# Cross attentions: ScalarE instead of VectorE copies the turned weighted sums, the outputs and, in the first one, the shift rows out of PSUM

## The reference

```python
def cross_of_layer_0(x, y):                  # heads of 32, softmax over 1500 context rows
    xn = ln(x) * lnx_g + lnx_b
    yn = ln(y) * lny_g + lny_b               # y is ctx_512
    q = einsum('bsc,hcd->bhsd', xn, wq)
    k = einsum('btc,hcd->bhtd', yn, wk)
    v = einsum('btc,hcd->bhtd', yn, wv)
    a = softmax(einsum('bhsd,bhtd->bhst', q, k) * 32 ** -0.5)
    o = einsum('bhst,bhtd->bhsd', a, v)
    ...                                      # output matrix, then an MLP

def cross_of_layer_1(q, k, v):               # heads of 8, k = v = ctx_512, with biases
    qh, kh, vh = (q @ Wq + bq), (k @ Wk + bk), (v @ Wv + bv)
    attn = softmax(einsum('bhqd,bhkd->bhqk', qh, kh) * 8 ** -0.5)
    return einsum('bhqk,bhkd->bhqd', attn, vh) @ Wo + bo
```

## Time and profile before

| | |
|---|---|
| median of 3 runs | 655.38 us (655.01 to 655.65) |
| the profiled execution | 658.64 us |
| its span | 656.8 us |
| `cross1`, first to last exponential | 120.1 to 317.2 us |
| `cross2`, first to last exponential | 424.6 to 619.7 us |
| PE busy | 612.1 us, 93% |
| DVE busy | 496.9 us, 76% |
| POOL busy | 380.3 us, 58% |
| ACT busy | 349.6 us, 53% |

### The profile page before, as it was taken

How to read it: one execution, slowest core, us unless ns; L and a number is a source line. 1 busy time by engine, 2 the same in 40 slices (tenths; PEclk the granted TensorE clock), 3 DMA queues, 4 the chain that set the end, 5 groups by cost and what they waited for, 6 DMA issues and landing times.

```text
span 656.8 us, 19531 instructions
## 1 busy us (share of the span) xinstructions
PE 612.1 (93%) x8614; PEld 458.6 (70%) x8614; DVE 496.9 (76%) x795; ACT 349.6 (53%) x540; POOL 380.3 (58%) x272
## 2 busy tenths in 40 slices
PE   9688898899999999999899889899999999999997
PEld 4466775677777777777776556677777777777864
DVE  3776738799989989896657764877988988988543
ACT  2245663655646646647263326276576586664442
POOL 1542453388888888574220325078988988955400
PEclk9879999999999999999899999999999999999998
DMA  4820003000000002000024000001101100000000
GB/s 162 232 122 2 4 1 136 1 2 2 2 2 2 2 3 96 3 2 2 1 84 170 1 0 1 1 2 49 49 2 50 49 2 2 2 2 2 2 1 15
DMA packets 4656, 20.85 MB, mean 32 GB/s; under 512 B 500, under 2 KB 756, under 8 KB 4572
## 3 DMA queue, kind: packets, MB, share of 16 engines
q1 hardware_dynamic: 4572, 19.60, 8.9%
HBM read 19.37 MB, written 0.23 MB: 30 GB/s over the span
## 4 chain that ended last, share of the span: by engine, by line
PE 71%; DVE 13%; ACT 8%; issue 5%; POOL 2%; DMA 1%; POOLq 0%; DVEq 0%; ACTq 0%
PE psum L1155 18%; PE psum L1053 10%; PE psum L1096 5%; PE psum L1103 5%; PE psum L1098 5%; PE psum L213 3%; DVE scratch L1277 3%; PE psum L1032 3%; PE psum L244 1%; PE psum L1072 1%; ACT scratch L1195 1%; POOL scratch L648 1%; PE psum L1059 1%; PE psum L1066 1%; ACT scratch L1193 1%
## 5 line engine op out<-in xcount | busy, mean ns | idle before, releaser
L1262 POOL TENSOR_TENSOR scratch<-scratch 125x896 bf16<-125x896 f32 x136 | 239.4, 1770 | 114.5 <-ACT scratch L1242 114.5
L1242 ACT ACTIVATE scratch<-psum 125x896 f32<-125x896 f32 x192 | 173.2, 915 | 146.4 <-PE psum L1155 145.2
L1277 DVE TENSOR_REDUCE scratch<-psum 128x1 f32<-128x500 f32 x336 | 209.9, 671 | 13.9 <-PE psum L1053 6.4
L1155 PE MATMUL psum<-scratch 128*125 128x448 bf16 (+2 forms) x624 | 143.7, 355 | 0.7 <-ACT scratch L1242 0.2
L1096 PE MATMUL psum<-tok,scratch 125*128 125x65 bf16 x1344 | 108.7, 195 | 2.3 <-DVE kT L1322 1.8
L1098 PE MATMUL psum<-tok,scratch 125*128 125x64 bf16 x1344 | 108.2, 192 | 0.0
L1096 PEld LDWEIGHTS psum<-tok,scratch 125*128 125x128 bf16 x1344 | 95.7, 97 | 15.5 <-issue 2.6
L1053 PE MATMUL psum<-scratch 128*128 128x500 bf16 x273 | 102.2, 375 | 3.1 <-DVE scratch L1277 2.0
L1098 PEld LDWEIGHTS psum<-tok,scratch 125*128 125x128 bf16 x1344 | 90.1, 98 | 16.1
L1155 PEld LDWEIGHTS psum<-scratch 128*125 128x125 bf16 (+2 forms) x624 | 79.6, 136 | 26.8 <-DVE scratch L1289 1.3
L1262 DVE TENSOR_TENSOR scratch<-scratch 125x896 bf16<-125x896 f32 x56 | 70.6, 1268 | 15.1 <-ACT scratch L1242 14.7
(11 more groups left out here) (340 smaller groups left out, 906.5 us busy)
## 6 DMA issues: line engine op xcount, KB each, us to landing
nrm<-turned_dram SPq DMA_DIRECT2D x8, 750.0 KB, 4.4
raw<-ctx_dram SPq DMA_DIRECT2D x4, 672.0 KB
w_third<-fifth_dram SPq DMA_DIRECT2D x3, 636.0 KB, 5.4
w_third<-third_dram SPq DMA_DIRECT2D x2, 844.0 KB, 8.4
w_third<-third_dram SPq DMA_DIRECT2D x2, 843.5 KB, 6.8
w_fourth<-fourth_dram SPq DMA_DIRECT2D x3, 542.5 KB, 5.9
w_first<-first_dram SPq DMA_DIRECT2D x1, 996.0 KB, 4.9
w_second<-second_dram SPq DMA_DIRECT2D x1, 834.5 KB, 6.9
```

What stands on the lines that cost most here:

```text
L1155: mm = nc.tensor.matmul(bank(S + f, HALF, CP), lhs[0:rows, CP * c:CP * c + CP], rhs[0:rows, HALF * f:HALF * f + HALF], start=(rows == 128) ...
L1242: nc.scalar.activation(CR["p"][0:CP, n % RING, :].rearrange("p (f n) -> p f n", f=2), psum[0:CP, S:S + 2, 0:HALF], ACT.Exp).then_inc(self. ...
L1262: ops.tensor_tensor(CR["pl"][0:CP, n % RING, :], CR["p"][0:CP, n % RING, :], p_high(n % RING), ALU.subtract).then_inc(done, 1)
L1277: nc.vector.tensor_reduce(mxp[:, r, t:t + 1], bank(B, TB), X_AXIS, ALU.max).then_inc(self.aux_freed, 1)
```

## The change

The readers of some units change engine, and with them the semaphore that frees the unit.

- N and O are read by ACT in both attentions (`on_act`, `copy_act`). The scale and bias of `cross1` go into the same ACT instruction.
- A is read by ACT in `cross1`; in `cross2` it stays with DVE.
- ACT does a unit where it does its units of that chunk: N and N behind the exponential of c = 3, O behind that of c = 5 (and behind the exponential alone, since `context_act` stands at c = 4 and 6), A and A behind that of c = 11. At the end of each attention it does the last N, N and O.
- A new semaphore `act_freed` counts what ACT has freed of these, and the waits of PE and POOL on such a unit count on it.
- The matmuls are the same ones in the same order.

```diff
+            def on_act(self, u):
+
+                return u[0] in ("NO" if self.biased else "NOA")
...
+                elif self.on_act(u):
+                    eng.wait_ge(self.act_freed, self.freed_by_act(idx))
...
+            def copy_act(self, act, u, idx, b):
+
+                kind, k = u
+                B, i = self.home(idx), b % 2
+                lo, hi = (0, 512) if k == 0 else (512, 896)
+                act.wait_ge(self.aux_ready, idx + 1)
+                if kind == "A":
+                    nc.scalar.activation(CR["qb", i][64:65, lo:hi], psum[64:65, B, 0:hi - lo], ACT.Copy
+                                         ).then_inc(self.act_freed, 1)
+                elif kind == "N":
+                    if k == 0 and b:
+                        act.wait_ge(self.aux_ready, self.index("O", 0, b - 1) + 1)
+                    if self is cross1:
+                        ins = nc.scalar.activation(usb[0:64, lo:hi], bank(B, hi - lo, 64), ACT.Identity,
+                                                   bias=col("lnyb", 0, 64), scale=col("lnyg", 0, 64))
+                    else:
+                        ins = nc.scalar.activation(usb[0:64, lo:hi], bank(B, hi - lo, 64), ACT.Copy)
+                    ins.then_inc(self.mean_turned, 1)
+                else:
+                    nc.scalar.activation(oT[:, :, 56 * b:56 * b + 56],
+                                         psum[:, B, 0:224].rearrange("p (j t) -> p j t", t=56), ACT.Copy
+                                         ).then_inc(self.act_freed, 1)
...
                     for unit in units:
                         self.act_unit(act, *unit)
+                for unit in self.last:
+                    self.act_unit(act, *unit)
...
-                elif kind == "N":
-                    dve.wait_ge(self.aux_ready, idx + 1)
...
-                        ins = nc.vector.tensor_copy(usb[0:64, lo:hi], bank(B, hi - lo, 64))
-                    ins.then_inc(self.mean_turned, 1)
-                elif kind == "O":
-                    dve.wait_ge(self.aux_ready, idx + 1)
-                    nc.vector.tensor_copy(oT[:, :, 56 * b:56 * b + 56],
-                                          psum[:, B, 0:224].rearrange("p (j t) -> p j t", t=56)
-                                          ).then_inc(self.aux_freed, 1)
...
-                for unit in self.last:
-                    self.dve_unit(dve, *unit)
...
+            for u in FRONT[-2:]:
+                cross1.copy_act(act, u, cross1.index(*u, 0), 0)
             cross1.run_act(act)
```

More of the change, by code:

```diff
@@ L952, in __init__ @@
                 self.tag, self.src, self.wk, self.wv, self.biased = tag, src, wk, wv, biased
[L953 removed]
+                (self.aux_ready, self.aux_freed, self.act_freed, self.scores, self.probs, self.pv_done, self.mean_turned, self.tok_high,
                  self.tok_set, self.ya_set, self.yb_set, self.q_high, self.max_set, self.rec_set, self.mean_set, self.low_dve,
@@ L956, in __init__ @@
                     sem(f"{tag}_{n}") for n in (
-                        "aux_ready", "aux_freed", "scores", "probs", "pv", "mean_turned", "tok_high", "tok_set",
+                        "aux_ready", "aux_freed", "act_freed", "scores", "probs", "pv", "mean_turned", "tok_high", "tok_set",
                         "ya_set", "yb_set", "q_high", "max_set", "rec_set", "mean_set", "low_dve", "low_pool",
@@ L977, in __init__, with freed_by_act @@
                 self.order += [(u, b) for u, _, b in self.last]
+            def on_act(self, u):
+                return u[0] in ("NO" if self.biased else "NOA")
             def freed(self, idx):
-                return sum(u[0] not in "TN" and (u[0], b) != ("Q", 0) for u, b in self.order[:idx + 1])
+                return sum(u[0] not in "TN" and not self.on_act(u) and (u[0], b) != ("Q", 0) for u, b in self.order[:idx + 1])
+            def freed_by_act(self, idx):
+                return sum(u[0] != "N" and self.on_act(u) for u, b in self.order[:idx + 1])
             def home(self, idx):
@@ L1168, in run_pe @@
                     pe.wait_ge(self.probs, CHUNKS * BATCH)
-                    projection(0, [HALVES[0]], self.aux_freed, self.freed(done))
-                    projection(1, [slice(N // 2, N - SEQ)], self.aux_freed, self.freed(done))
+                    projection(0, [HALVES[0]], self.act_freed, self.freed_by_act(done))
+                    projection(1, [slice(N // 2, N - SEQ)], self.act_freed, self.freed_by_act(done))
                 if projection is None:
@@ L1189, in act_unit @@
                     if k == 0 and b >= 2:
-                        act.wait_ge(self.aux_freed, self.freed(self.index("A", 1, b - 2)))
+                        self.wait_freed(act, self.index("A", 1, b - 2))
                     cols = slice(HALF * k, HALF * k + HALF)
@@ L1285, in dve_unit @@
                     shift, below = CR["qb", i][64:65, lo:hi], psum[64:65, B, 0:hi - lo]
-                    if self.biased:
-                        if b < 2:
-                            dve.wait_ge(y_ones, 7)
-                        nc.vector.tensor_tensor(shift, below, CR["qb", i][96:97, lo:hi], ALU.subtract
-                                                ).then_inc(self.aux_freed, 1)
-                    else:
-                        nc.vector.tensor_copy(shift, below).then_inc(self.aux_freed, 1)
+                    if b < 2:
+                        dve.wait_ge(y_ones, 7)
+                    nc.vector.tensor_tensor(shift, below, CR["qb", i][96:97, lo:hi], ALU.subtract
+                                            ).then_inc(self.aux_freed, 1)
                 elif kind == "T":
@@ L1351, in front_dve_run @@
                         self.front_low_dve(dve, 1)
-                    self.dve_unit(dve, u, k + self.turns + 2, 0)
+                    if not self.on_act(u):
+                        self.dve_unit(dve, u, k + self.turns + 2, 0)
             def run_dve(self, dve, projected=None):
@@ L1356, in run_dve @@
                     b, c = n // CHUNKS, n % CHUNKS
-                    units = list(itertools.chain(*self.steps[b][c]))
+                    units = [u for u in itertools.chain(*self.steps[b][c]) if not self.on_act(u[0])]
                     if c == LAG - 1 and b:
@@ L1412, in total_units @@
             def total_units(self):
-                return self.freed(len(self.order) - 1)
+                return self.freed_by_act(len(self.order) - 1)
         ln_b = sig("norms_b_dve", ["xb0", "xn0", "xb1", "xn1"])
```

17 lines of the change are left out of this document (5 added, 12 removed).

## The result

The changed kernel takes 658.2 us, the median of 13 runs (656.31 to 663.0). The kernel before, run beside it on the same chip, takes 655.65 us (13 runs, 652.98 to 658.25). The ratio is 1.0054 with a 95% interval of 1.0027 to 1.0080: slower by 3.5 us, between 1.8 and 5.2. The ratio is not the quotient of the two medians, which are 2.55 us apart. The forecast was slower by 5.0 us, 660.4; the time lies exactly on the lower end of its range (658.2 to 663.2).

What follows compares the result with a forecast made beforehand. PE was taken as the bound, held in the second attention by a gapless POOL that ACT feeds. Terms 5.5 - 0.6 + 0.2 + 0.2 - 0.3 = +5.0 us on 655.4 gave 660.4 us, range 658.2 to 663.2.

Steps and rivals of the forecast that it cites:

- step 1: `cross2`, rounds 1 to 5: N copies delay exponential 5, POOL and PE by 1.10 us each (0.9 to 1.2); +5.5 us.
- step 5: A and the rest of `cross1`: ACT has the shift row about as early as DVE, POOL's slack covers N; nothing.
- step 2: `cross2`, rounds 2 to 5: later PE no longer waits for DVE's low part of chunk 11; -0.6 us.
- step 3: `cross2`, round 6: PE's second and third maxima wait for the N copies; +0.2 us, hidden in rounds 1 to 5.
- step 4: O behind exponential 5: covered in middle rounds; in the last round of `cross1` exponential 6 comes later, +0.2 us once.
- step 6: Behind each attention, where copies stand alone: shorter on ACT, with the first shift row -0.3 us (-0.5 to 0).
- A: Rival: POOL's lateness in `cross2` doesn't reach PE, through hidden slack or catching up; 656.2 us, no change; chance 0.10.
- B: Rival: DVE takes the shared ports from POOL at low part 10, up to 4.0 us more, 664.4 us; chance 0.12.
- C: Rival: DVE is the bound, its maxima start earlier without N and the kernel ends faster, 652 us; chance 0.04.

Runs made afterwards that it cites:

- c2_o: Changed kernel with only O of the second attention on ACT, the rest as before: loop of `cross2` 194.15 us (before 194.23, after 197.82).
- c1_a: Changed kernel with only A of the first attention on ACT, the rest as before: loop of `cross1` 195.26 us (before 196.13).
- c1_no: Changed kernel with only N and O of the first attention on ACT, the rest as before: loop of `cross1` 196.18 us (before 196.13).
- act_pad: Kernel before plus one unused 64x448 ACT copy behind exponential 3, rounds 1 to 5 of `cross2`: its loop 195.71 us, 1.48 longer.

## Why the prediction was right, and where its size was off

By the loops the change is -0.88 + 3.59 = +2.7 us, with the ends of both attentions some 0.1 less; the runs give +3.5 (1.8 to 5.2). The forecast was +5.0. Sign, place and mechanism hold, the sizes of its steps less so: both large errors, in steps 1 and 5, made the forecast too slow. That the time is still in the range is partly luck. It lies on its lower end, outside the forecast's own bounds (659.2 to 662.3), and by the loops the change is smaller than the 3.5 to 6.5 us that had a chance of 0.74.

1. **The N copies, +5.5 forecast, +4.1 measured** (five times the 0.82 us of round 1, which has nothing of step 2). The mechanism is as written, seen in every link: ACT's row, the gap of 0.81 us ahead of low part 5, no gap behind it, PE's wait at chunk 10 in five rounds. The mis-sized term is the price of a copy in the row. I added durations, 0.591 + 0.487. The durations were right: 582 and 479 ns in the rows below. But one instruction on ACT starts before the one ahead of it has ended. From start to start it is 0.82 us from exponential 3 to the first copy, 0.47 from there to the second and 0.37 to exponential 4, together 1.66 where it was 0.81. So the copies cost 0.85 and not 1.10, in five rounds 1.3 us less. The earlier trace rows had shown this overlap: exponential 4 starts 0.81 us after an exponential of 0.92. I used it for the exponentials and not for the copies. My lower bound of 0.9 was too high for the same reason.
2. **DVE's low part of chunk 11, -0.6 forecast, -0.6 measured.** Round 1, which has no such wait, is 0.82 us longer; rounds 2 to 5 by 0.68, 0.69, 0.65 and 0.65, together 0.61 less than four times 0.82. The stall itself was 0.14 to 0.16 us in each of them and is gone. Right.
3. **The maxima in round 6, +0.2 forecast, +0.13 measured.** In round 3 the second and third maxima start 1.45 and 1.88 us after exponential 3, where the earlier trace rows have 1.33 and 1.76: PE is held up once by 0.12, not twice.
4. **O, +0.2 in the last round of `cross1`, +0.04 measured.** The row's error again: behind exponential 5 O takes 0.23 us from start to start, and exponential 6 follows 1.03 us after 5, where the earlier trace rows have 0.99. In the middle rounds nothing, as forecast (c2_o).
5. **A, nothing forecast, -0.88 measured.** This step failed. I compared A's price on the two engines and asked what stands behind it on ACT. I didn't ask what stands behind it on DVE: the low part of chunk 11, which begins 1.1 us sooner against its exponential (0.96 us after it, was 2.05) and with that gets out of POOL's way. c1_a alone shows all of it. N of `cross1` costs nothing, as forecast: with N and O alone the loop is 0.05 us longer (c1_no), which is O's.
6. **The ends, -0.3 forecast, about -0.1 seen.** From the start of the last exponential to the first output matmul behind the last O it is 6.92 us in `cross2`, was 7.00, and 11.84 in `cross1`, was 11.89. In `cross1` the copies with scale and bias are hardly shorter on ACT (763 and 660 ns) than on DVE (796 and 661).

The groups behind steps 1 and 6, by line and shape, of the changed kernel (busy us, mean ns):

```profile
L1228 ACT ACTIVATE scratch<-psum,w_second 64x512 f32<-64x512 f32 x8 | 6.1, 763 | 8.3 <-PE psum L1076 8.3
L1228 ACT ACTIVATE scratch<-psum,w_second 64x384 f32<-64x384 f32 x8 | 5.3, 660 | 0.0
L1231 ACT ACTIVATE scratch<-psum 64x512 f32<-64x512 f32 x8 | 4.7, 582 | 3.5 <-PE psum L1076 3.5
L1231 ACT ACTIVATE scratch<-psum 64x384 f32<-64x384 f32 x8 | 3.8, 479 | 0.2 <-PE psum L1076 0.2
```

With 0.85 in step 1, the measured steps 2, 3 and 6, and -0.88 for the loop of `cross1` (steps 4 and 5 together), the forecast's own sum comes to 4.25 - 0.6 + 0.1 - 0.9 - 0.1 = +2.75 us, where loops and ends say +2.6.

The rivals. **A** (POOL's lateness doesn't reach PE) falls with PE's five waits, and with act_pad. **B** (DVE takes the ports from POOL) falls too: POOL's low part 10 took 1.67 us, and it was DVE's low part 11, begun at 523.93 behind POOL's low part and the cast that follows it, that took 1.50. POOL did pay once, where nobody waits: its token difference at 524.57 took 1.62 us, was 0.90, and it still idles 1.9 us before the next chunk 3. **C** (DVE is the bound) falls: DVE lost 8.5 us of busy time in the loop of `cross2` (158.6 to 150.1), and the loop grew by 3.6.

What stays open: by the ratio the changed kernel is 3.5 us slower, by the medians 2.55, by loops and ends 2.6. The interval holds all three, and one stretch at the lower clock outside the loops, 1.3 to 1.7 us, is more than what they differ by.

## What to carry to other kernels

Before work is moved to an idle engine, look at the row that it joins: an engine at 53% had a gapless row of 3.3 us that fed another engine with no slack for 13 us, and of 0.85 us put there 0.82 came out at the end of round 1. Price an instruction within such a row by the distance of starts, not by its duration, and look at both ends of a move, also at what comes earlier on the engine that is left. Where a late start costs time, slack further down the chain can be the cheaper cure: one reordered operation on POOL gave back 4.6 us (1.1 of it in a round that the change hadn't touched), while taking work off POOL ahead of the late start gave nothing.

## What the runs showed of the hardware

- Instructions on ACT that stand ready one behind the other overlap by about 0.1 us: copies out of PSUM of 512 and 384 columns last 0.582 and 0.479 us, but the next one starts 0.47 and 0.37 us after them; O of 224 columns lasts 0.34 and takes 0.23; a copy of 448 columns within SBUF lasts 0.56 and takes 0.46.
- A scale and a bias, one value for each partition, cost ACT 0.18 us in each copy out of PSUM: 763 against 582 ns at 512 columns, 660 against 479 at 384. On DVE they cost 796 against 675 and 661 against 541 ns.
- Between DVE and POOL 0.03 us decide who pays: POOL's difference of 0.89 us took 1.81 when DVE's low part had begun 0.03 us ahead of it. The price can be reckoned. The second one lasts its own time and what is left of the first, less 0.14 us: 1.06 + 0.89 - 0.14 = 1.81 here, 0.72 + 1.09 - 0.14 = 1.67 for DVE's low part at 197.45, 0.86 + 0.90 - 0.14 = 1.62 for POOL's difference at 524.57. Of the 127 meetings of a low part of DVE with work of POOL in the loops of both traces, 122 fit this within 0.02 us.
- The other five belong to one event, that stands in rounds 1 to 4 of the changed `cross2`. POOL was in low part 10 when DVE's low part 11 began (523.93), and POOL's cast behind it (523.98, 0.50 us) was still ahead of DVE: 0.55 us are left to the end of the cast, and 0.55 + 1.09 - 0.14 = 1.50. There the operation that began first was not the first to be served.
